# A routed expert layer: token lists by packed place from one-hot products instead of rows scattered to padded places

## The reference, cut to what matters

```python
scores = jax.nn.softmax(xf @ Wg, axis=-1)            # 4096 tokens, 32 experts
weights, indices = jax.lax.top_k(scores, TOP_K)      # TOP_K = 4
...
for e in range(E):
    pos = jnp.nonzero(pair_expert == e, size=C, fill_value=P)[0]
    ...
    out = swiglu(xf[tok], W1[e], W2[e], W3[e]) * w[:, None]
    y = y.at[tok].add(out)
z = swiglu(xf, Ws1, Ws2, Ws3)                        # shared expert
return (y + z).reshape(B, S, D)
```

## Time and profile before

| what | us |
|---|---|
| median of 3 runs | 2562.9 (2553.0 to 2563.3) |
| profiled execution, whole | 2555.9 |
| its span in the trace | 2554.1 |
| attention and correlation stages | 0 to 368 |
| routed layer, first block | 368.6 to 590 |
| routed layer, second block (160 tiles) | 590 to 847 |
| second decoder layer | 847 to 2554 |

### The profile page before, as it was taken

The page is one execution under the profiler, slowest core; times in us unless marked ns, Lnnn a source line. Parts: engine busy times, 40 slices in busy tenths (PEclk is TensorE's granted clock), DMA queues, the critical chain, the costliest instruction groups (busy, mean ns, idle before and its releaser), DMA issues. The chain is left out here.

```text
span 2554.1 us, 40576 instructions
## 1 busy us (share of the span) xinstructions
PE 2217.9 (87%) x12182; PEld 1521.4 (60%) x12183; DVE 1336.1 (52%) x2971; ACT 785.3 (31%) x1695; POOL 884.7 (35%) x1090
## 2 busy tenths in 40 slices
PE   6999857767999576888888896999999999999997
PEld 3445534446999332333333333655579899998996
DVE  5553354344666475777677774479423333333332
ACT  2222312212333114655556664322211111111111
POOL 1100215667000536445543110122224444444443
PEclk9999977878999768999999999999999999999998
DMA  9997126224666535334542121310048888888885
GB/s 316 372 369 256 34 79 239 102 96 143 180 179 179 145 83 121 74 73 107 110 97 66 47 68 62 123 42 17 17 125 267 271 260 260 263 268 265 268 261 161
DMA packets 272711, 412.86 MB, mean 162 GB/s; under 512 B 32023, under 2 KB 226303, under 8 KB 272618
## 3 DMA queue, kind: packets, MB, share of 16 engines
q1 hardware_dynamic: 233962, 352.06, 42.5%
q0 software_dynamic: 38656, 59.70, 11.0%
HBM read 262.18 MB, written 148.89 MB: 161 GB/s over the span
## 5 line engine op out<-in xcount | busy, mean ns | idle before, releaser
L2659 PE MATMUL me_hp<-me_xgT,me_w 128*128 128x160 f32 x3072 | 436.6, 302 | 1.1 <-DVE me_xgT L2697 0.6
L2659 PEld LDWEIGHTS me_hp<-me_xgT,me_w 128*128 128x128 f32 x3072 | 421.4, 191 | 24.2 <-issue 22.8
L1393 DVE TENSOR_REDUCE hd_nmax<-hd_wide 128x2 f32<-128x1024 f32 x256 | 307.7, 1219 | 128.1 <-PE hd_wide L1131 125.0
L1322 ACT ACTIVATE hd_prob<-hd_slim 128x512 f32<-128x512 f32 x512 | 276.3, 602 | 191.2 <-PE hd_slim L1142 157.7
L2727 DVE TENSOR_TENSOR me_hid<-me_act_out,me_hp 128x160 f32<-128x160 f32 x384 | 123.3, 321 | 334.2 <-ACT me_act_out L2683 284.0
L2683 ACT ACTIVATE me_act_out<-me_hp 128x160 f32<-128x160 f32 x384 | 116.4, 303 | 558.6 <-PE me_hp L2659 467.1
L1142 PE MATMUL hd_slim<-hd_q_stack,hd_k_stack 100*128 100x512 bf16 x512 | 199.5, 393 | 39.9 <-ACT hd_prob L1322 33.5
L1131 PE MATMUL hd_wide<-hd_k_stack,hd_q_stack 97*128 97x512 bf16 x512 | 201.1, 397 | 32.2 <-DVE hd_rest L1387 15.9
L2028 PEld LDWEIGHTS mr_e_hp<-mr_e_xtT,mr_e_w_now 128*128 128x128 f32 x1280 | 169.3, 193 | 8.3 <-ACT mr_e_xtT L2048 0.2
L2028 PE MATMUL mr_e_hp<-mr_e_xtT,mr_e_w_now 128*128 128x128 f32 x1280 | 170.1, 276 | 0.0
L2314 PE MATMUL me_r_hp<-me_r_xnT,me_r_sw 128*128 128x512 f32 x384 | 167.5, 592 | 0.0
(11 more groups left out here) (384 smaller groups left out, 3607.0 us busy)
## 6 DMA issues: line engine op xcount, KB each, us to landing
me_w<-in_L_ffn_w_exp SPq DMA_DIRECT2D x192, 512.0 KB
places<-z_zero SPq DMA_DIRECT2D x64, 1152.0 KB, 11.1
me_w_first<-in_L_ffn_w_exp SPq DMA_DIRECT2D x32, 768.0 KB
me_w_second<-in_L_ffn_w_exp SPq DMA_DIRECT2D x32, 768.0 KB
mr_e_xt<-places SPq DMA_DIRECT2D x160, 144.0 KB, 2.3
outputs<-mr_e_y SPq DMA_DIRECT2D x160, 128.0 KB, 1.9
part_rows<-hd_parts SPq DMA_DIRECT2D x48, 256.0 KB
hd_k_stack<-part_rows SPq DMA_DIRECT2D x192, 64.0 KB
```

The source lines that it names most:

```text
L1322: nc.scalar.activation(prob[:, u, :], slim[:, slim_slot(bt, item), :], ACT.Exp, scale=D ** -0.5)\
L1393: nc.vector.tensor_reduce(nmax[:, g % 2, n // 2, c:c + 2], wide[:, at], AX.X, ALU.max, negate=True)\
L2659: last = nc.tensor.matmul(hp[:, f % 3, half * CAP:(half + 1) * CAP], w1[:, sl, c, cols], xgT[:, sl, c, :], start=(c == 0), stop=(c == DC - 1))
```

## The change

No row is scattered and nothing is filled with zeros, but for one tile of `outputs`. DVE keeps the ranks of all batches (`ranked_rows`). After the last batch it has the first packed row of each expert (`first_rows`) and, in four groups of eight tiles, the packed row of each pair, split into tile number and lane (`placing`). Then a list of tokens is made for each packed place: for each of the 32 tiles, DVE makes a one-hot of the tile number (128 x 4 x 160), POOL subtracts the lane from 0..127 (128 x 4 x 128), ACT squares that and takes Relu(number - number x square), which is the token's number at its own lane and 0 elsewhere, and TensorE multiplies the two and sums in PSUM. DVE casts the sum to `token`, and POOL gathers the rows of each of the 160 tiles by it, eight ahead of the loop and one in each of its steps. POOL also makes the normalised rows, and SP stores them once, in order, to `routed_rows`, between the loads of the weights.

```diff
+        def gather(pool, n):
+            nc.gpsimd.indirect_dma_start(out=xt[:, n % UNROLL, :], out_offset=None, in_=rows_out[:, :],
+                                         in_offset=bass.IndirectOffsetOnAxis(ap=token[:, n:n + 1], axis=0)).then_inc(x_loaded[n % UNROLL], 16)
...
-                    for n in range(0, E, 8):
...
+                    for b in range(B):
+                        sp.wait_ge(rows_ready, b * TB + TB)
+                        sp.wait_ge(gated, b + 1)
+                        sp.dma_start(rows_out[b * S:(b + 1) * S, :].rearrange("(j p) n -> p j n", p=P), xg[:, b % SLOTS])\
+                            .then_inc(stored[b % SLOTS], 16)
+                        if b < B // 2:
+                            es = slice(b * (2 * E // B), (b + 1) * (2 * E // B))
...
                     for b in range(B):
-                        pool.wait_ge(placed, b + 1)
...
-                                nc.gpsimd.indirect_dma_start(
-                                    out=places[:, :], out_offset=bass.IndirectOffsetOnAxis(ap=place[:, b * TB + j, n:n + 1], axis=0),
-                                    in_=xg[:, b % SLOTS, j, :], in_offset=None).then_inc(scattered[b % SLOTS], 16)
...
+                        if b >= SLOTS:
+                            pool.wait_ge(stored[b % SLOTS], 16 * (b // SLOTS))
...
+                            nc.gpsimd.tensor_scalar(xg[:, b % SLOTS, j, 0:D], x[:, t, :], mean[:, t:t + 1], rstd[:, t:t + 1],
+                                                    ALU.subtract, ALU.mult).then_inc(rows_ready, 1)
+                    for t in range(NT):
+                        pool.wait_ge(lanes_ready, t // GROUP + 1)
+                        if t >= ONES:
+                            pool.wait_ge(listed, t - ONES + 1)
+                        nc.gpsimd.tensor_tensor(at_lane[:, t % ONES], lanes[:].unsqueeze(1).to_broadcast([P, TOP, P]),
+                                                lane_f[:, t, :].unsqueeze(2).to_broadcast([P, TOP, P]), ALU.subtract).then_inc(lane_off, 1)
...
+                    pool.wait_ge(tokens_ready, 1)
+                    for n in range(UNROLL):
+                        gather(pool, n)
...
+                    for t in range(NT):
+                        pe.wait_ge(lane_numbered, t + 1)
+                        pe.wait_ge(tile_made, t + 1)
+                        for n in range(TOP):
+                            last = nc.tensor.matmul(turned_list, at_lane[:, t % ONES, n, :], at_tile[:, t % ONES, n, :],
+                                                    start=(t == 0 and n == 0), stop=(t == NT - 1 and n == TOP - 1))
+                        last.then_inc(listed, 1)
...
+                        nc.scalar.activation(lane, lane, ACT.Square).then_inc(lane_squared, 1)
...
+                        nc.scalar.activation(lane, lane, ACT.Relu, bias=number[:, t:t + 1], scale=less_number[:, t:t + 1])\
+                            .then_inc(lane_numbered, 1)
...
+                    def tiles_of(t):
+
+                        if t >= ONES:
+                            dve.wait_ge(listed, t - ONES + 1)
+                        nc.vector.tensor_tensor(at_tile[:, t % ONES], tile_nos[:].unsqueeze(1).to_broadcast([P, TOP, TILES]),
+                                                tile_f[:, t, :].unsqueeze(2).to_broadcast([P, TOP, TILES]), ALU.is_equal).then_inc(tile_made, 1)
...
                 @block.gpsimd
                 def _(pool):
-                    chain = Chain(pool, shifted)
...
+                    for n in range(UNROLL, TILES):
+                        pool.wait_ge(y_ready, n - UNROLL + 1 + 2)
+                        gather(pool, n)
...
-                with sp.Fori(0, n_tiles // ROWS) as i:
-                    sp.dma_start(places[bass.ds(i * (ROWS * P), ROWS * P), :].rearrange("(j p) d -> p j d", p=P), zero[:])\
-                        .then_inc(cleared, 16)
```

More of the change, by code:

```diff
@@ L1783, in _ @@
                         second(b)
[L1784 to L1787, removed]
+                    for t in range(NT):
[5 more added lines that the diff above has]
+                        last.then_inc(listed, 1)
+                        if t == 2 * GROUP:
+                            pe.wait_ge(tabled, 1)
+                            for n in range(2):
+                                last = nc.tensor.transpose(tp[0:1, n * P:(n + 1) * P], table[:, n:n + 1], ident[:])
+                            last.then_inc(table_turned, 1)
                 @block.scalar
@@ L1851, in choice, with ranking @@
                         dve.sem_inc(sel_ready, 1)
-                    def placing(b):
+                    def ranking(b):
                         dve.wait_ge(rank_full, b + 1)
                         chain.link(nc.vector.scalar_tensor_tensor(chosen[:], ranks, float(CAP), chosen[:], ALU.is_le, ALU.mult))
[L1857 to L1866, removed]
@@ L1880, in add, with first_rows @@
                         last.then_inc(y_free, 1)
+                    def first_rows():
+                        dve.wait_ge(counted, 1)
+                        chain.link(nc.vector.tensor_scalar(count[:], counts, float(CAP), None, ALU.min))
+                        chain.link(nc.vector.tensor_tensor(over, count[:].unsqueeze(2).to_broadcast([P, E, PER]),
+                                                           steps_of[:].unsqueeze(1).to_broadcast([P, E, PER]), ALU.is_gt))
+                        chain.link(nc.vector.tensor_reduce(tiles[:], over, AX.X, ALU.add))
+                        chain.link(nc.vector.tensor_tensor_scan(ends[:], ones[:, 0:E], tiles[:], 0.0, ALU.mult, ALU.add))
+                        chain.link(nc.vector.tensor_tensor(first_row[:], ends[:], tiles[:], ALU.subtract))
+                        chain.link(nc.vector.tensor_scalar(first_row[:], first_row[:], float(P), None, ALU.mult))
@@ L1959, in _ @@
                 def _(pool):
-                    chain = Chain(pool, shifted)
-                    flat = place_f[:].rearrange("p t n -> p (t n)")
-                    chain.link(nc.gpsimd.tensor_scalar(moved[:], flat, shift_by[:, 0:1], None, ALU.add))
-                    for e in range(1, E + 1):
-                        chain.link(nc.gpsimd.tensor_scalar(step[:], flat, float(CAP * e), shift_by[:, e:e + 1], ALU.is_ge, ALU.mult))
-                        chain.link(nc.gpsimd.tensor_tensor(moved[:], moved[:], step[:], ALU.add))
@@ L2763, in program @@
         x_loaded = [k.sem(f"x_loaded{n}") for n in range(4)]
-        scattered = [k.sem(f"scattered{j}") for j in range(TB)]
         gathered = [k.sem(f"gathered{j}") for j in range(TB)]
@@ L2799, in program @@
             place = r.sb("place", [P, NT, TOP], I32)
-            mix_experts_routed(nc, second, x, ident, stats, mean, rstd, a["L0_ffn_Wg"], a["L0_ffn_w_in"], a["L0_ffn_w_out"], places, outputs,
-                               scattered, place, first)
+            mix_experts_routed(nc, second, x, ident, stats, mean, rstd, a["L0_ffn_Wg"], a["L0_ffn_w_in"], a["L0_ffn_w_out"],
+                               scratch["routed_rows"], outputs, place, first)
             first.close()
```

188 lines of the change are left out of this document (93 added, 95 removed).

## The result

The changed kernel takes 2604.2 us (median of 4, 2599.3 to 2609.3) against 2560.9: ratio 1.0175, 95% interval 1.0143 to 1.0206. I had forecast 2562 and a range to 2598. Its profiled execution has a span of 2600.3 us, 46.2 more than before.

What follows compares the result with a forecast made beforehand. TensorE was taken to bound the tile loop, POOL's scatters the first block (163 of 222 us). Scatters and stalls given back, against list, gathers and rows, gave about 1 us less: 2555, plus 7 for the median, 2562; range 2538 to 2598.

Steps and rivals of the forecast that it cites:

- Steps 1 to 5: Path up to the tile loop's first transpose: it starts at 592.4, against 593.39 before, -1.0 us.
- 1: First batch, POOL making rows: 1.1 us a row, bounds 0.72 and 1.6; second batch's logits at 395.6.
- 2: First block, batches without scatters: six more cycles of 15.0 us, to 485.6; bounds 14.6 and 25.
- 3: Last batch, `first_rows` and first group's `placing`: batch done at 502.3, list starts at 507.2.
- 4: Token list: POOL and DVE exclude each other, 1.80 a tile, 73.2 us; bounds -16 (1.35 a tile) and +15.
- 5: From the list's end to the first transpose: cast 0.3, eight gathers 10.2, barrier and first instructions 1.5 us.
- likeliest case: Whole kernel: the prediction's own case, POOL and DVE excluding each other in the list, range 2550 to 2574; 42%.
- Step 6: Tile loop: POOL's gather, 1.27 us a tile, lies beside TensorE's 1.586 and costs nothing, unless POOL is held up.
- third rival: Tile loop: DVE's `w_now` holds up gathers (16 us), or remote waits enter unrolled ends (10 to 20); 2578 to 2598; 13%.
- second rival: Token list: TensorE's clock, at 1.2 GHz, paces it, +0.47 us a tile, 15 us, 2577; 15%.
- fourth: First block: remote waits come from something else than scatters, seven batches keep 9 us each, +63, 2625; 7%.
- No exclusion: Token list: POOL and DVE do not hold each other up, 1.35 us a tile, 16 us less, 2546; 20%.

Runs made afterwards that it cites:

- e2: Kernel before, with one indirect gather of 1152-byte rows a tile added to its loop from tile 40, into an unread tile: 2600.5 us, loop 287.9.
- r4: Changed kernel with POOL's gathers in a hardware loop, run again beside the unaltered changed kernel: 2594.1 us, loop 297.5.
- e12: Changed kernel, DVE making only 8 of 160 one-hot columns from the fourth list tile on: 2582.2 us.
- e13: Changed kernel with more slack in the tile loop, DVE's rows for two batches and 16 slots for gathered rows: 2580.6 us (1.0052), loop 286.3.
- e14: The kernel of e13 with a 0.2 us POOL operation between gathers: 2564.5 us (0.999 against the kernel before), loop 271.3.

## Why the prediction was wrong, by its steps

**Steps 1 to 5 were right to 5.4 us in their sum,** partly by luck: the list was 6.9 shorter than forecast, while the stretch behind it was 3.0 longer and the whole block started 3.8 late. The changed kernel's rows behind them, from the timeline and the source view:

```profile
L1734 POOL TENSOR_SCALAR mr_s_xg<-all_x,all_mean,all_rstd x32: 1208/1212/1229, 375.1 to 442.5; 128x256 f32<-128x256 f32 x32
```
```profile
571.94 0.33 DVE L1985 CAST mr_token<-mr_s_lp 128x160 int32<-128x160 f32 x1 [3.61 <-PE mr_s_lp L1824]
573.22 1.23 POOL L1627 DMA_INDIRECT mr_xt<-routed_rows,mr_token  x1 [4.23 <-DVE mr_token L1985]
...
582.26 0.95 POOL L1627 DMA_INDIRECT mr_xt<-routed_rows,mr_token  x1 [0.30 <-issue]
...
586.97 0.45 PE L2047 MATMUL mr_e_xp<-all_ident,mr_xt 128*128 128x128 f32 x1 [15.06 <-PEq L1695]
```

| step | forecast | measured |
|---|---|---|
| 1: a row on POOL | 1.1 | 1.21 |
| 1: second batch's logits | 395.6 | 397.7, in a block that started 3.8 later |
| 2: a batch | 15.0 | 14.5 |
| 3: list starts | 507.2 | 505.6 |
| 4: a tile's pair of POOL and DVE | 1.80 | 1.6 |
| 4: the list | 73.2 | 66.3 |
| 5: cast to first transpose | 12.0 | 15.0, of it 3.8 for the barrier (taken 1.5) |
| first transpose | 592.4 | 587.0 |

The scatters' removal took the remote waits along, as I had read. The likeliest case was right in mechanism on the list, too: POOL and DVE hold each other up. But a tile costs 1.04 + 0.57, not 0.98 + 0.82, since DVE starts 0.11 us ahead of POOL and not all of what is left of its operation is lost. The 0.98 itself stands in no row of before; with the 1.27 that the step names, the pair would have been 2.09 and the list 9 us longer still. It was near the measured 1.04 by luck. The bound of -16 is also not what its 1.35 gives (32 x 0.45 = 14.4), which changes nothing here.

**Step 6 failed**, the sentence "Nothing, unless POOL is held up (a rival)" on the gathers of the tile loop. The loop with them was 46.0 us longer, of 46.2 in all. I had counted POOL's time and the lead of the gathers, both rightly (a gather and its gap are 1.25 us, and TensorE hardly waited for rows), and had also found that in the first block indirect DMAs come with stalls of ACT and DVE of 9 us a batch. I took these for something of long straight-line code ("a loop's body is short") and so did not carry them to the loop, where more such DMAs run (152 against 128). e2 shows that waits come with added gathers in the loop, too, and r4 that they stay when POOL's own code is a short loop.

**The third rival** had the right place and too small a price: 2578 to 2598. Its second half, waits that come along into the loop, is what happened, but all through the loop and for 46 us, not at its unrolled ends for 10 to 20. Its first half is refuted. A gather in the loop took 0.946 us in the median, just its usual time, though DVE's `w_now` ran over many of them. By the Trainium skill, page SBUF — State Buffer, section Who interferes with whom, such a copy locks descriptor generation out; no run here shows that. What the rows do show is the reverse and small: `w_now` took 0.47 us in the mean, against 0.42 before.

**The second rival** fell: TensorE was at 0.87 of its clock in the list, and POOL at 1.6 a tile paced it. **The fourth** fell, with no remote wait left. **No exclusion** fell by e12: with DVE's part cut to a twentieth, the list was 12 us shorter.

**The fill** cost nothing, as said. That the first block began 3.8 us later is no effect of it: over all kernels run here its first operation of ACT starts between 370.2 and 375.1 us, in those that fill with zeros and in those that don't. The 6.6 us behind the loop stay open: outside the group at 2515 this part took 1705.4 to 1715.0 us in the kernels with the change, and 1705.7 to 1708.8 in the four traces without it.

**What stays open:** what it is that holds ACT up. Shown is that it comes with POOL's indirect DMAs, whether they move 1152 or 64 bytes a row, in all groups but one, and that it is worse where they follow each other closely (11 us in the loop on one chip, 15 on another). Whether ACT stands still or the signal of TensorE's product reaches it late, no run told apart. That the loop of e13 is still 33 us longer than before, with slack of two tiles more, speaks for more than a late signal to ACT; that in e14 DVE, too, starts 2.54 us behind a finished product of TensorE speaks against a fault of ACT alone.

## What to carry to other kernels

Moving indirect DMAs off the critical path doesn't make them free: price them by what they did to the other engines where they ran, and not only by POOL's own time. Before a cure is believed, run the uncured kernel beside it on the same chip: here two cures seemed to give 36 us, and 11 and 3 of them were theirs (the 3 from one execution each, where two of the changed kernel differ by 1.4). And a loop in which TensorE is busy for 99.5% of the time has no slack for waits of 2 us; slack, lead and distance together gave back 28 us of 46.

## What the runs showed of the hardware that I had not expected

- A chip on which the kernel before takes 2515.3 us (7 runs, 2513.7 to 2519.9), where the others have 2553 to 2575, and on which none of the four kernels with gathers had a long wait of ACT (the changed kernel as it is did not run there): the same kernel's loop is 263.4 there and 289.2 elsewhere. Whether the 45 us of the kernel before are its remote waits was not seen, since it left no trace there.
- With at most two gathers under way, the loop took 310.5/160 = 1.94 us a tile, with 99.7 us of POOL's waits for their landing.
- Gathers of 64 bytes a row cost POOL (0.947 us) and the loop (291.0) as much as those of 1152 bytes (0.945, 287.9).
